# Six tiles of the first layer ahead of the expert steps and two between them, instead of four and four; gates, splits and the last output moved to fit

## The chip, the cores and the metric

One core of one Trainium2 chip. The metric is the device time of one execution in microseconds (us), smaller is better. The engines are TensorE (PE in the rows; PEld is its weight load), VectorE (DVE), ScalarE (ACT), GpSimd (POOL) and SyncE (SP, which here only issues DMAs).

## The reference

The kernel computes two residual layers over x of 32 batches x 128 tokens x 128 channels, all float32:

```python
# layer 0: low-rank conditioned linear, exact gelu; u = v = fside (128 x 16 per batch)
z  = einsum('bfr,bor->bfo', einsum('bfi,bir->bfr', x, v) / 128, u) / 16
x  = x + gelu(x @ W.T + fc_bias + z + cond[:, None, :])
# layer 1: four experts and a shared one, top 2 of 4 per batch
gate_logits = gate_in(means of x over token ranges) @ gate_w + gate_b
gate_logits = gate_logits * (1 + scale) + shift      # scale, shift from silu(cond)
w_be = top-2 weights of softmax(gate_logits)         # one weight per batch and expert
for e in range(4):
    h = gelu_tanh(x @ ew1[e] + eb1[e])               # 128 -> 512
    out += w_be[:, e] * mask[e] * (h @ ew2[e] + eb2[e])  # 512 -> 128
x  = x + out + gelu_tanh(x @ sw1 + sb1) @ sw2 + sb2
```

`mask` leaves a third of the tokens out for experts 2 and 3.

## The kernel before

The 32 batches are 8 tiles of 4 batches, 512 columns each. Every engine has its program written out by hand, so the order of calls in the Python code is the order of each engine's queue, and semaphores tie the queues together.

**Layer 0 of a tile** is `xT` and `transpose_F` (PE transposes of x and of fside), their copies on ScalarE (`xT_copy`, `fT_copy`), `matrices` (PE: F F^T per batch), `matrix` (VectorE, L666: adds W^T), `layer0` (PE, L515), `gelu0` (ScalarE, L355) and `residual` (VectorE, L673). Then x1 is cut into a high part (`x1_high`, ScalarE, L389) and a low part (`x1_low`, VectorE, L678), since every large product is made of three matmuls (`product3`: high x high, high x low, low x high; L456, L457, L458). Weights are cut in the same way: `weight_high` (ScalarE, L330) and `weight_low` (VectorE, L691), ten arrays in the order `WEIGHTS`.

**Steps.** A step k is one tile t with one expert s (0 is the shared one), in the order `STEPS`; there are 40. `first_step(t)` is 2, 7, 12, 17, 22, 27, 32, 36. `up(k)` makes the four 128-row chunks of the hidden layer on PE, `gelu(k)` takes them through ScalarE, `split(k)` cuts them on VectorE (for s = 0 L701 and L705, otherwise L711 and L716, four of each), `down(k)` multiplies back on PE. PE runs `up(k + 2)` ahead of `down(k)`. Five PSUM banks form a ring for `up`.

**Early and late tiles.** The first `NA` = 4 tiles go through layer 0 before `up(0)`; with their own PSUM banks. Tile t >= NA is *late*: its pieces stand between steps, the first at step `first_step(t - NA)` (`late_tile(k, place)` gives the tile whose piece at this place is due in step k), and all of them share PSUM bank 7. Since exact gelu and tanh gelu sit in two function tables of ScalarE, each late tile costs it two table loads (L361 and L380).

**Gates.** `segment_sums` (VectorE, L685) sums x1 over token ranges, `time_gate` and `gate_in` prepare, `logits` (PE, L583) sums over channels, `modulation` reads the product of the conditioning, `gate_logits` and `gate_weights` (VectorE) rank and weigh, `gate_tanh` (ScalarE) is between them. Group 0 is tiles 0 to 3, then 4-5 and 6-7; `late_gate` places the later two. Every `split` of an expert needs the weights `w_be` of its tile.

**Output of a tile:** `out_sum` (VectorE, L728), `out_transpose` (PE, L569), `out_copy` (ScalarE, L398), then a DMA from SP.

`keep_busy` (L462) issues matmuls on ones, whose result is not used. The chunks of x are `CHUNKS` = tiles 0, 1, 2-3, 4-5, 6-7, numbered 0 to 4.

Of the kernel before, what the change touches and what calls it, by code (L numbers as in the profile page):

```python
# [12 lines left out]
def build(nc, x, fside, cond, W, fc_bias, gate_w, gate_b, time_w, time_b,  # L13
# [4 lines left out]
    NB = 4  # L18
# [28 lines left out]
    NA = 4  # L47
# [6 lines left out]
    with ExitStack() as ctx:  # L54
# [122 lines left out]
        psOut = ps[:, 7, :]  # L177

# [55 lines left out]
        def _(sp):  # L234
# [26 lines left out]
            load_weight(WEIGHTS[0])  # L261
            sp.dma_start(b1_rows[0:CH, :], sb1.rearrange("(c p) -> c p", c=CH)).then_inc(b1_in, 16)
            sp.dma_start(b1_rows[CH:NS * CH, :], eb1.rearrange("e (c p) -> (e c) p", c=CH)).then_inc(b1_in, 16)
            for dst, src in (
                    (gate_raw[:, :, :], gate_w.rearrange("(g d) e -> d g e", g=3)),
                    (gate_b_row[:, :], gate_b.rearrange("(a e) -> a e", a=1).to_broadcast([128, E])),
                    (time_w_raw[:, :], time_w)):
                sp.dma_start(dst, src).then_inc(gate_loads_in, 16)
            load_weight(WEIGHTS[1])
            for n in WEIGHTS[2:]:  # L270
                load_weight(n)
            for c in (3, 4):
                load_F(c)
                load_x(c)
            for t in range(NT):
# [3 lines left out]
            sp.wait_ge(out_left, 16 * NT)  # L279
# [40 lines left out]
        def _(act):  # L320
# [91 lines left out]
            for t in range(NA):  # L412
# [4 lines left out]
                if t >= 1:  # L417
                    x1_high(t - 1)
                if t >= 2:
                    weight_high(WEIGHTS[t - 2])  # L420
            x1_high(NA - 1)
            weight_high(WEIGHTS[2])
            weight_high(WEIGHTS[3])
            act.wait_ge(b1_ok, 1)
            gelu(0)
            gate_tanh(0)
            gelu(1)
            for n in WEIGHTS[4:6]:
                weight_high(n)
            for k in range(2, K):  # L430
# [5 lines left out]
                if s == NS - 1:  # L436
                    out_copy(t)
                t = late_tile(k, 2)
# [12 lines left out]
            out_copy(NT - 1)  # L451

        @block.tensor
        def _(pe):
# [186 lines left out]
            out_transpose(NT - 1)  # L641

        @block.vector
        def _(dve):
# [74 lines left out]

            def out_sum(t):  # L720
# [49 lines left out]
            def gate_in(g):  # L770
                b = batches(g)
                n = GATES[g][1] - GATES[g][0]
                dve.wait_ge(segsum_ok, NSEG * GATES[g][1] // 2)
# [66 lines left out]
            for t in range(NA):  # L840
# [3 lines left out]
                if t >= 1:  # L844
                    x1_low(t - 1)
                if t == 2:
                    output_rows()
                    weight_low(WEIGHTS[0])
                    segment_sums(0, 2)
            segment_sums(2, 4)  # L850
            time_gate()
            gate_in(0)
            x1_low(NA - 1)
            dve.wait_ge(bias_in, 16 * 3)
            modulation()
            weight_low(WEIGHTS[1])
            weight_low(WEIGHTS[2])
            gate_logits(0)
            split(0)
            gate_weights(0)  # L860
            weight_low(WEIGHTS[3])
            split(1)
            weight_low(WEIGHTS[4])
            weight_low(WEIGHTS[5])
            for k in range(2, K):
# [7 lines left out]
                if k == 4:  # L873
                    output_biases(0)
                t = late_tile(k, 2)
# [23 lines left out]
            out_sum(NT - 1)  # L899
# [24 lines left out]
```

## Time and profile before

| | us |
|---|---|
| median of 3 runs | 264.66 (263.34 to 264.92) |
| profiled execution | 262.98 |
| its span | 261.3 |
| PE busy in the span | 240.2 (92%) |
| DVE busy | 196.7 (75%) |
| ACT busy | 145.0 (55%) |
| mean granted TensorE clock | 0.993 |

The span runs from the first to the last instruction; 1.7 us of the profiled execution lie around it. Matmuls overlap in the records, so the steps' pace is read from the starts of rows, not from their durations.

### The profile page before, as it was taken

How to read it: one execution, taken by the hardware profiler on the slowest of the kernel's cores; microseconds unless marked ns; L12 is line 12 of the kernel's file. 1: busy time of each engine (PE TensorE's matmuls, PEld its weight loads, DVE VectorE, ACT ScalarE, POOL GpSimd, SP SyncE). 2: the span in 40 equal slices, each digit the busy share in tenths (PEclk: the TensorE clock that was granted, in tenths of full speed). 3: DMA queues.
4: the chain of work that ended last, by engine and by line, in shares of the span. 5: the costliest groups of instructions: out<-in, count | busy, mean ns of one | idle time of the engine just before them, and what ended most of it. 6: DMA issues, size and time to landing. Idle time of an engine off the chain costs nothing.

```text
span 261.3 us, 3479 instructions
## 1 busy us (share of the span) xinstructions
PE 240.2 (92%) x1230; PEld 200.7 (77%) x1230; DVE 196.7 (75%) x450; ACT 145.0 (55%) x270; POOL 15.1 (6%) x39
## 2 busy tenths in 40 slices
PE   8987788999899998999899998998989989999963
PEld 7875466888688877888678877886778879898852
DVE  0259899997689546977796966995799859679761
ACT  3478795353976089552966269544735175545500
POOL 6000000004000020002000020002000100010000
PEclk9999979999999999999999999999999999999999
DMA  6997000000000000100001000100000000100101
GB/s 129 219 292 144 1 0 3 0 0 0 3 21 19 0 3 1 40 3 0 0 1 43 0 0 1 43 0 0 0 17 25 0 0 14 29 0 1 40 3 40
DMA packets 17100, 7.41 MB, mean 28 GB/s; under 512 B 5523, under 2 KB 16443, under 8 KB 17083
## 3 DMA queue, kind: packets, MB, share of 16 engines
q1 hardware_dynamic: 16069, 6.98, 10.8%
q10 hardware_dynamic: 854, 0.18, 0.3%
q8 instruction: 10, 0.16, 0.3%
q0 software_dynamic: 160, 0.02, 0.1%
q14 instruction: 7, 0.06, 0.1%
HBM read 5.09 MB, written 2.10 MB: 28 GB/s over the span
## 4 chain that ended last, share of the span: by engine, by line
PE 67%; ACT 14%; DVE 14%; issue 3%; DVEq 0%; POOL 0%; ACTq 0%; POOLq 0%
PE ps L456 20%; PE ps L458 18%; PE ps L457 18%; ACT h L380 5%; PE ps L503 3%; DVE hs_lo L716 3%; ACT hs_hi L383 3%; DVE hs_lo L705 2%; ACT L380 2%; DVE hs_hi L711 2%; PE ps L473 2%; PE ps L462 2%; PE ps L487 2%; ACT L361 1%; PE ps L569 1%
## 5 line engine op out<-in xcount | busy, mean ns | idle before, releaser
L380 ACT ACTIVATE h<-ps,b_col 128x512 f32<-128x512 f32 (+1 forms) x160 | 92.4, 642 | 64.1 <-PE ps L458 49.4
L716 DVE SCALAR_TENSOR_TENSOR hs_lo<-h,w_be,hs_hi 128x512 fp32r<-128x512 f32 (+1 forms) x128 | 76.2, 656 | 0.0
L456 PE MATMUL ps<-x_hi,W_hi 128*128 128x512 f32 (+1 forms) x160 | 64.3, 402 | 8.2 <-ACT hs_hi L383 4.9
L456 PE MATMUL ps<-hs_hi,W_hi 128*128 128x512 f32 (+1 forms) x160 | 59.2, 370 | 5.2 <-DVE hs_lo L716 2.5
L457 PE MATMUL ps<-x_hi,W_lo 128*128 128x512 f32 (+1 forms) x160 | 59.1, 369 | 0.0
L458 PE MATMUL ps<-x_lo,W_hi 128*128 128x512 f32 (+1 forms) x160 | 59.0, 369 | 0.0
L458 PE MATMUL ps<-hs_lo,W_hi 128*128 128x512 f32 (+1 forms) x160 | 58.5, 365 | 0.0
L457 PE MATMUL ps<-hs_hi,W_lo 128*128 128x512 f32 (+1 forms) x160 | 58.2, 363 | 0.0
L711 DVE TENSOR_SCALAR hs_hi<-h,w_be 128x512 fp32r<-128x512 f32 (+1 forms) x128 | 48.2, 440 | 12.7 <-PE ps L458 6.7
L456 PEld LDWEIGHTS ps<-x_hi,W_hi 128*128 128x128 f32 x160 | 30.4, 190 | 20.4 <-ACT hs_hi L383 10.9
L456 PEld LDWEIGHTS ps<-hs_hi,W_hi 128*128 128x128 f32 x160 | 30.1, 188 | 10.9 <-DVE hs_lo L716 2.8
L458 PEld LDWEIGHTS ps<-x_lo,W_hi 128*128 128x128 f32 x160 | 30.5, 190 | 4.4
L457 PEld LDWEIGHTS ps<-hs_hi,W_lo 128*128 128x128 f32 x160 | 30.1, 188 | 4.0
L458 PEld LDWEIGHTS ps<-hs_lo,W_hi 128*128 128x128 f32 x160 | 30.1, 188 | 4.1
L457 PEld LDWEIGHTS ps<-x_hi,W_lo 128*128 128x128 f32 x160 | 30.6, 192 | 2.9
L315 POOL TENSOR_TENSOR x<-x,bias 128x168 f32<-128x168 f32 (+1 forms) x24 | 11.1, 490 | 213.4 <-DVE hs_lo L716 159.9
L701 DVE CAST hs_hi<-h 128x1024 fp32r<-128x1024 f32 x8 | 5.5, 693 | 20.2 <-ACT h L380 20.2
L398 ACT ACTIVATE x_tok<-ps 128x512 f32<-128x512 f32 x8 | 4.8, 599 | 27.4 <-PE ps L569 27.4
L705 DVE TENSOR_TENSOR hs_lo<-h,hs_hi 128x1024 fp32r<-128x1024 f32 x16 | 18.8, 1218 | 0.0
L334 ACT ACTIVATE x<-ps 128x512 f32<-128x512 f32 x8 | 4.8, 598 | 15.0 <-PE ps L473 15.0
L383 ACT ACTIVATE hs_hi<-ps,b_col 128x512 fp32r<-128x512 f32 x16 | 11.0, 689 | 0.0
L666 DVE SCALAR_TENSOR_TENSOR h<-ps,WT 128x512 f32<-128x512 f32 x4 | 2.7, 687 | 9.3 <-PE ps L503 9.3
(106 smaller groups left out, 175.4 us busy)
## 6 DMA issues: line engine op xcount, KB each, us to landing
W_raw<-in_L_cond_ew SPq DMA_DIRECT2D x8, 256.0 KB, 5.5
out<-x_tok SPq DMA_DIRECT2D x8, 256.0 KB, 2.3
x_tok<-in_x SPq DMA_DIRECT2D x6, 168.0 KB
x_tok<-in_x SPq DMA_DIRECT2D x3, 176.0 KB
W_raw<-in_L_cond_sw SPq DMA_DIRECT2D x2, 256.0 KB, 4.6
x_tok<-in_x SPq DMA_DIRECT2D x3, 84.0 KB
F_raw<-in_fside_Bx1x1024x SPq DMA_DIRECT2D x3, 64.0 KB, 4.7
x_tok<-in_x SPq DMA_DIRECT2D x2, 88.0 KB
```

Source lines behind the costliest of these rows:

```text
L315: nc.gpsimd.tensor_tensor(xb[:, :, at:at + n], xb[:, :, at:at + n], bias2[:, i, t * NB:(t + 1) * NB].unsqueeze(2).to_broadcast([128, NB, n ...
L380: ins = nc.scalar.activation(span(h[:, k % 3, c, :], s), up_bank(k, c), ACT.Gelu_apprx_tanh, bias=b1_col[:, s, c:c + 1])
L383: ins = nc.scalar.activation(hs_hi[:, k % 2, c, :], up_bank(k, c), ACT.Gelu_apprx_tanh, bias=b1_col[:, s, c:c + 1])
L456: nc.tensor.matmul(dst, w_hi, m_hi, start=start, stop=False)
L457: nc.tensor.matmul(dst, w_lo, m_hi, start=False, stop=False)
L458: return nc.tensor.matmul(dst, w_hi, m_lo, start=False, stop=stop)
L462: nc.tensor.matmul(dst, ones[:, :], ones[:, :], start=True, stop=True)
L503: last = nc.tensor.matmul(dst[:, b * D:(b + 1) * D], f[:, b, :], f[:, b, :], start=True, stop=True)
L701: nc.vector.tensor_copy(hs_hi[:, k % 2, CH // 2:, :], h[:, k % 3, CH // 2:, :]).then_inc(shared_hi_ok, 1)
L705: nc.vector.tensor_tensor(hs_lo[:, k % 2, c:c + 2, :], h[:, k % 3, c:c + 2, :], f32(hs_hi[:, k % 2, c:c + 2, :]), ALU.subtract).then_inc(l ...
L711: nc.vector.tensor_scalar(hs_hi[:, k % 2, :, c], h[:, k % 3, :, c], w_be[:, t * NB + b, s - 1:s], None, ALU.mult).then_inc(hi_ok, 1)
L716: nc.vector.scalar_tensor_tensor(hs_lo[:, k % 2, :, c], h[:, k % 3, :, c], w_be[:, t * NB + b, s - 1:s], f32(hs_hi[:, k % 2, :, c]), ALU.m ...
```

## The change

- `NA` becomes 6: tiles 4 and 5 go through layer 0 ahead of `up(0)`, tiles 6 and 7 are late, at steps 2 and 7 on. The gate groups are unchanged, but `late_gate` puts group 1 (tiles 4-5) at steps 3 to 9 instead of 13 to 19, and group 2 (tiles 6-7) at 13 to 19 instead of 23 to 29.
- SP issues the loads in another order: the small loads, then the first weight, then chunk 3 of x and fside, then the other weights, then chunk 4.
- ScalarE makes x1_high of tiles 0 and 1 only in the front; those of tiles 2 and 3 come around `gelu(1)`, those of 4 and 5 after `gelu(4)` and `gelu(5)`. `gelu(1)` now stands ahead of `gate_tanh(0)`, and the weights are cut elsewhere.
- VectorE makes `time_gate` in the front, sums the segments of tiles 0 to 3 in one call (three instructions) and of 4-5 in another, and has `weight_low` and `x1_low` at other places.
- The last tile's output goes in two halves of two batches each, with a PSUM bank, a copy and a DMA for each.

```diff
--- before.py
+++ after.py
@@ -44,7 +44,7 @@
     AT = {step: k for k, step in enumerate(STEPS)}
     RING = [0, 1, 4, 2, 3]
 
-    NA = 4
+    NA = 6
 
     GATES = [(0, 4), (4, 6), (6, 8)]
 
@@ -175,6 +175,7 @@
         psIdle = ps[:, 3, 0:128]
         psY = [ps[:, 5, :], ps[:, 6, :]]
         psOut = ps[:, 7, :]
+        psLast = [psOut, ps[:, RING[0], :]]
 
         block = ctx.enter_context(nc.Block())
 
@@ -258,7 +259,6 @@
             load_x(1)
             load_F(2)
             load_x(2)
-            load_weight(WEIGHTS[0])
             sp.dma_start(b1_rows[0:CH, :], sb1.rearrange("(c p) -> c p", c=CH)).then_inc(b1_in, 16)
             sp.dma_start(b1_rows[CH:NS * CH, :], eb1.rearrange("e (c p) -> (e c) p", c=CH)).then_inc(b1_in, 16)
             for dst, src in (
@@ -266,17 +266,24 @@
                     (gate_b_row[:, :], gate_b.rearrange("(a e) -> a e", a=1).to_broadcast([128, E])),
                     (time_w_raw[:, :], time_w)):
                 sp.dma_start(dst, src).then_inc(gate_loads_in, 16)
+            load_weight(WEIGHTS[0])
+            load_F(3)
+            load_x(3)
             load_weight(WEIGHTS[1])
             for n in WEIGHTS[2:]:
                 load_weight(n)
-            for c in (3, 4):
-                load_F(c)
-                load_x(c)
-            for t in range(NT):
+            load_F(4)
+            load_x(4)
+            for t in range(NT - 1):
                 sp.wait_ge(out_tok_ok, t + 1)
                 sp.dma_start(out[t * NB:(t + 1) * NB, :, :].rearrange("b l d -> l b d"), x_tok[:, t, :, :]
                              ).then_inc(out_left, 16)
-            sp.wait_ge(out_left, 16 * NT)
+            for half in range(2):
+                b = (NT - 1) * NB + half * NB // 2
+                sp.wait_ge(out_tok_ok, NT + half)
+                sp.dma_start(out[b:b + NB // 2, :, :].rearrange("b l d -> l b d"),
+                             x_tok[:, NT - 1, half * NB // 2:(half + 1) * NB // 2, :]).then_inc(out_left, 16)
+            sp.wait_ge(out_left, 16 * (NT + 1))
 
         @block.gpsimd
         def _(pool):
@@ -414,17 +421,18 @@
                     xT_copy(t + 2)
                     fT_copy(t + 2)
                 gelu0(t)
-                if t >= 1:
+                if t in (1, 2):
                     x1_high(t - 1)
-                if t >= 2:
-                    weight_high(WEIGHTS[t - 2])
-            x1_high(NA - 1)
-            weight_high(WEIGHTS[2])
-            weight_high(WEIGHTS[3])
+                if t in (3, 5):
+                    weight_high(WEIGHTS[t // 4])
             act.wait_ge(b1_ok, 1)
             gelu(0)
+            for n in WEIGHTS[2:4]:
+                weight_high(n)
+            x1_high(2)
+            gelu(1)
             gate_tanh(0)
-            gelu(1)
+            x1_high(3)
             for n in WEIGHTS[4:6]:
                 weight_high(n)
             for k in range(2, K):
@@ -435,6 +443,8 @@
                 t, s = STEPS[k - 3] if k >= 3 else (0, 0)
                 if s == NS - 1:
                     out_copy(t)
+                if k in (4, 5):
+                    x1_high(k)
                 t = late_tile(k, 2)
                 if t is not None:
                     fT_late_copy(t)
@@ -448,7 +458,11 @@
                 g = late_gate(k, 7)
                 if g is not None:
                     gate_tanh(g)
-            out_copy(NT - 1)
+            for half in range(2):
+                b = slice(half * NB // 2, (half + 1) * NB // 2)
+                act.wait_ge(out_ps, NT + half)
+                nc.scalar.activation(x_tok[:, NT - 1, b, :], psLast[half].rearrange("p (b d) -> p b d", d=D)[:, b, :],
+                                     ACT.Copy).then_inc(out_tok_ok, 1)
 
         @block.tensor
         def _(pe):
@@ -638,7 +652,18 @@
                 t, s = STEPS[k - 1] if k >= 1 else (0, 0)
                 if s == NS - 1:
                     out_transpose(t)
-            out_transpose(NT - 1)
+
+            t = NT - 1
+            for half in range(2):
+                pe.wait_ge(outT_ok, NSEG * (t + 1 + half))
+                if half == 0:
+                    pe.wait_ge(out_tok_ok, t)
+                else:
+                    pe.wait_ge(h_ok, CH * K)
+                for b in range(half * NB // 2, (half + 1) * NB // 2):
+                    last = nc.tensor.transpose(psLast[half][:, b * D:(b + 1) * D], outT[:, t % 2, b * L:(b + 1) * L],
+                                               ident[:, :])
+                last.then_inc(out_ps, 1)
 
         @block.vector
         def _(dve):
@@ -717,6 +742,19 @@
                                                    w_be[:, t * NB + b, s - 1:s], f32(hs_hi[:, k % 2, :, c]),
                                                    ALU.mult, ALU.subtract).then_inc(lo_ok, 1)
 
+            def last_sum(half):
+                t = NT - 1
+                b = slice(half * NB // 2, (half + 1) * NB // 2)
+                dst_v, sum_v, x1_v = (ap.rearrange("p (b l) -> p b l", l=L)
+                                      for ap in (outT[:, t % 2, :], psY[t % 2], x1[:, t, :]))
+                if half == 0:
+                    dve.wait_ge(down_ok, AT[t, NS - 1] + 1)
+                    dve.wait_ge(x1b_ok, NSEG * NT)
+                    dve.wait_ge(out_ps, t - 1)
+                for at, dst, n in SEGS:
+                    nc.vector.tensor_tensor(dst_v[:, b, dst:dst + n], sum_v[:, b, at:at + n], x1_v[:, b, at:at + n],
+                                            ALU.add).then_inc(outT_ok, 1)
+
             def out_sum(t):
                 dve.wait_ge(down_ok, AT[t, NS - 1] + 1)
                 dve.wait_ge(x1b_ok, NSEG * (t + 1))
@@ -770,7 +808,7 @@
             def gate_in(g):
-                dve.wait_ge(segsum_ok, NSEG * GATES[g][1] // 2)
+                dve.wait_ge(segsum_ok, NSEG * (g + 1))
                 linked(nc.vector.tensor_tensor(gate_terms[:, :, b, :],
                                                segsum[:, :, b].unsqueeze(3).to_broadcast([128, NSEG, n * NB, E]),
                                                gw[:, :, :].unsqueeze(2).to_broadcast([128, NSEG, n * NB, E]), ALU.mult))
@@ -841,25 +879,29 @@
                 if t + 1 < NA:
                     matrix(t + 1)
                 residual(t)
-                if t >= 1:
+                if t in (1, 2):
                     x1_low(t - 1)
+                if t == 1:
+                    time_gate()
                 if t == 2:
                     output_rows()
+                if t == 3:
+                    segment_sums(0, 4)
+                if t == 4:
                     weight_low(WEIGHTS[0])
-                    segment_sums(0, 2)
-            segment_sums(2, 4)
-            time_gate()
+            segment_sums(4, 6)
             gate_in(0)
-            x1_low(NA - 1)
             dve.wait_ge(bias_in, 16 * 3)
             modulation()
             weight_low(WEIGHTS[1])
+            gate_logits(0)
             weight_low(WEIGHTS[2])
-            gate_logits(0)
             split(0)
+            weight_low(WEIGHTS[3])
             gate_weights(0)
-            weight_low(WEIGHTS[3])
+            x1_low(2)
             split(1)
+            x1_low(3)
             weight_low(WEIGHTS[4])
             weight_low(WEIGHTS[5])
             for k in range(2, K):
@@ -872,6 +914,8 @@
                     weight_low(WEIGHTS[2 * k + 3])
                 if k == 4:
                     output_biases(0)
+                if k in (6, 7):
+                    x1_low(k - 2)
                 t = late_tile(k, 2)
                 if t is not None:
                     matrix(t)
@@ -896,7 +940,8 @@
                 g = late_gate(k, 7)
                 if g is not None:
                     output_biases(g)
-            out_sum(NT - 1)
+            last_sum(0)
+            last_sum(1)
 
 
 # ---- launch: one core; inputs and output as the reference has them ----
```

`late_tile` and `late_gate` and the pieces that they place are the same code as before.

The order of VectorE's queue in the front, before the change, from tile 1's residual sum on (`h` is the matrix of layer 0, `x` is x1):

```order
L673 TENSOR_TENSOR x<-x,h 128x512
L678 TENSOR_TENSOR x_lo<-x,x_hi 128x512
L666 SCALAR_TENSOR_TENSOR h<-ps,WT 128x512
L673 TENSOR_TENSOR x<-x,h 128x512
L678 TENSOR_TENSOR x_lo<-x,x_hi 128x512
L752 COPY eb2T<-ps 128x4 x3
L754 COPY b_col<-ps 128x20
L756 MEMSET eb2T 128x1
L757 MEMSET eb2T 128x1
L691 TENSOR_TENSOR W_lo<-W_raw,W_hi 128x512
L685 TENSOR_REDUCE segsum<-x 128x8 x3
L673 TENSOR_TENSOR x<-x,h 128x512
```

The same queue after the change, from the matrix of tile 4 to the gate's input:

```order
L691 SCALAR_TENSOR_TENSOR h<-ps,WT 128x512
L698 TENSOR_TENSOR x<-x,h 128x512
L710 TENSOR_REDUCE segsum<-x 128x16 x3
L691 SCALAR_TENSOR_TENSOR h<-ps,WT 128x512
L698 TENSOR_TENSOR x<-x,h 128x512
L716 TENSOR_TENSOR W_lo<-W_raw,W_hi 128x512
L698 TENSOR_TENSOR x<-x,h 128x512
L710 TENSOR_REDUCE segsum<-x 128x8 x3
L812 TENSOR_TENSOR gate_terms<-segsum,gw 128x3x64
L815 TENSOR_REDUCE gate_fold<-gate_terms 128x64
```

The sums over four tiles (128x16) now stand between the residual sum of tile 3 and the matrix of tile 5, and two residual sums and a second group of sums stand ahead of the gate's input.

ScalarE's queue ahead of the first tanh gelu, before the change (`x_hi` is x1_high, the gelu of layer 0 is the row with `bias`):

```order
L355 ACTIVATE h<-ps,bias 128x128 x4
L389 ACTIVATE x_hi<-x 128x512
L330 ACTIVATE W_hi<-W_raw 128x512
L389 ACTIVATE x_hi<-x 128x512
L330 ACTIVATE W_hi<-W_raw 128x512 x2
L380 ACT_TABLE_LOAD
L380 ACTIVATE h<-ps,b_col 128x512
```

and after it:

```order
L362 ACTIVATE h<-ps,bias 128x128 x4
L337 ACTIVATE W_hi<-W_raw 128x512
L362 ACTIVATE h<-ps,bias 128x128 x8
L337 ACTIVATE W_hi<-W_raw 128x512
L387 ACT_TABLE_LOAD
L387 ACTIVATE h<-ps,b_col 128x512
```

One cut of a weight is left between the last gelu of layer 0 and the table load, in place of three cuts of weights and two of x1.

VectorE's queue between the weights of gate 0 (`w_be`) and the split of step 2, before:

```order
L817 TENSOR_TENSOR w_be<-denom,sum_top 128x64
L691 TENSOR_TENSOR W_lo<-W_raw,W_hi 128x512
L701 CAST hs_hi<-h 128x1024
L705 TENSOR_TENSOR hs_lo<-h,hs_hi 128x1024 x2
L691 TENSOR_TENSOR W_lo<-W_raw,W_hi 128x512 x2
L711 TENSOR_SCALAR hs_hi<-h,w_be 128x4x128 x4
```

and after:

```order
L855 TENSOR_TENSOR w_be<-denom,sum_top 128x64
L703 TENSOR_TENSOR x_lo<-x,x_hi 128x512
L726 CAST hs_hi<-h 128x1024
L730 TENSOR_TENSOR hs_lo<-h,hs_hi 128x1024 x2
L703 TENSOR_TENSOR x_lo<-x,x_hi 128x512
L716 TENSOR_TENSOR W_lo<-W_raw,W_hi 128x512 x2
L736 TENSOR_SCALAR hs_hi<-h,w_be 128x4x128 x4
```

Two cuts of x1 have come into this stretch; the weight cut that stood in it is now ahead of the gate's weights.

## Rows read from the trace of the kernel before

**Rows 1.** Window, us; busy us (x count) of PE, PEld, DVE, ACT, POOL; clock, DMA share, GB/s.

```profile
20.00:60.00 40.00, 35.13 (x163) 27.43 (x162) 38.70 (x98) 25.73 (x48) 1.35 (x3) 0.96 0.11 22
```

**Rows 2.** Window of the first loads, same columns.

```profile
2.00:9.00 7.00, 6.94 (x42) 5.90 (x40) 0.69 (x1) 3.25 (x6) 3.12 (x7) 1.00 0.94 186
```

**Rows 3.** Timeline of the front: start us, us, engine, line, operation [idle before <-releaser].

```profile
11.74 1.06 PE L515 MATMUL ps<-x,h 128*128 128x128 f32 x8
...
14.74 1.06 PE L515 MATMUL ps<-x,h 128*128 128x128 f32 x8
...
18.14 1.14 ACT L355 ACTIVATE h<-ps,bias 128x128 f32<-128x128 f32 x4 [0.64 <-PE ps L515]
...
19.01 1.13 PE L515 MATMUL ps<-x,h 128*128 128x128 f32 x8 [0.91 <-issue]
...
19.98 1.50 PE L462 MATMUL ps<-ones 128*128 128x128 f32 x12
...
21.73 0.50 PE L456 MATMUL ps<-x_hi,W_hi 128*128 128x512 f32 x1 [0.25 <-DVE W_lo L691]
```

**Rows 4.** Timeline from the segment sums to the first gate, same columns.

```profile
24.04 1.33 DVE L685 TENSOR_REDUCE segsum<-x 128x8 f32<-128x336 f32 x3
...
25.25 1.28 ACT L380 ACT_TABLE_LOAD   x1
...
26.54 0.69 ACT L380 ACTIVATE h<-ps,b_col 128x512 f32<-128x512 f32 x1
...
29.25 1.29 DVE L691 TENSOR_TENSOR W_lo<-W_raw,W_hi 128x512 fp32r<-128x512 f32 x2
...
30.88 0.22 DVE L784 TENSOR_TENSOR logit<-ps,gate_mul 128x64 f32<-128x64 f32 x1 [0.34 <-PE ps L583]
```

**Rows 5.** Timeline of split and down of step 2.

```profile
45.90 2.73 DVE L716 SCALAR_TENSOR_TENSOR hs_lo<-h,w_be,hs_hi 128x512 fp32r<-128x512 f32 x4
...
48.77 0.47 PE L456 MATMUL ps<-hs_hi,W_hi 128*128 128x512 f32 x1
```

**Rows 6.** Timeline of split and down of steps 6 (no gate) and 16 (gate 1).

```profile
66.61 0.69 DVE L701 CAST hs_hi<-h 128x1024 fp32r<-128x1024 f32 x1 [2.86 <-ACT h L380]
...
72.92 0.39 PE L456 MATMUL ps<-hs_hi,W_hi 128*128 128x512 f32 x1
...
125.87 0.69 DVE L701 CAST hs_hi<-h 128x1024 fp32r<-128x1024 f32 x1 [3.63 <-ACT h L380]
...
132.71 0.50 PE L456 MATMUL ps<-hs_hi,W_hi 128*128 128x512 f32 x1 [0.37 <-DVE outT L728]
```

**Rows 7.** Timeline, the output transposes of tiles 0 to 5.

```profile
75.69 0.60 PE L569 MATMUL ps<-ident,outT 128*128 128x128 f32 x4
...
105.31 0.60 PE L569 MATMUL ps<-ident,outT 128*128 128x128 f32 x4
...
135.57 0.60 PE L569 MATMUL ps<-ident,outT 128*128 128x128 f32 x4
...
165.23 0.60 PE L569 MATMUL ps<-ident,outT 128*128 128x128 f32 x4
...
193.35 0.60 PE L569 MATMUL ps<-ident,outT 128*128 128x128 f32 x4
...
219.58 0.60 PE L569 MATMUL ps<-ident,outT 128*128 128x128 f32 x4
```

**Rows 8.** Timeline of the end.

```profile
256.39 0.82 DVE L728 TENSOR_TENSOR outT<-ps,x 128x168 f32<-128x168 f32 x3 [3.12 <-PE ps L458]
...
258.58 0.37 SPq L277 DMA_DIRECT2D out<-x_tok  x1
```

**Rows 9.** Windows around the clock's fall (columns of Rows 1).

```profile
32.00:33.00 1.00, 0.00 (x0) 0.00 (x0) 0.97 (x3) 1.00 (x3) 0.00 (x0) 1.00 0.00 0
...
35.00:36.00 1.00, 1.00 (x3) 0.80 (x3) 1.00 (x2) 1.00 (x3) 0.00 (x0) 0.50 0.00 0
...
252.00:253.00 1.00, 0.00 (x0) 0.00 (x0) 1.00 (x2) 0.00 (x0) 0.00 (x0) 1.00 0.00 0
```

## The prediction

> **What bounds the kernel now.** I read the engines' shares first: PE is busy 92% of the span, VectorE 75%, ScalarE 55%, so by the average PE sets the time. Then the windows, because the average is over stages with different limits. Two stages must be told apart. From 20 to 60 us VectorE is busy 38.7 of 40 us and PE 35.1 [rows 1]: this stage belongs to VectorE, which cuts ten weights and four tiles, works out the first gate and starts the splits, all at once. Its last word is step 2: the split of step 2 ends at 45.90 + 2.73 = 48.63 us, and down(2) starts at 48.77 [rows 5]. From there on PE runs without such waits and sets the pace; a block of five steps (from one output transpose to the next) takes 29.62, 30.26, 29.66, 28.12 and 26.23 us [rows 7]. The first three hold a late tile, the fourth a gate without one, the fifth neither. So the sum has three parts: how much later PE reaches the start of down(2), what each block loses or gains, and the end.
>
> **Part 1, the front: when does down(2) start?** I follow the queues, each on the durations of before.
>
> *PE to the layer-0 product of tile 3.* In the front a tile costs PE 3.0 us: the products of tiles 0 and 1 start at 11.74 and 14.74 [rows 3], with the next tile's transposes between them. Now such transposes follow tile 1 too; at 3.0 a tile, tile 2's starts at 17.7, tile 3's at 20.7 and ends at 21.9 (1.13 to 1.16 each). In the kernel before, tile 3's starts at 19.01 [rows 3]. VectorE and ScalarE keep up to here: time_gate adds some 1.3 us to VectorE's queue at tile 1, where it would wait anyway, and its matrix of tile 3 is then ready by about 20.2.
>
> *The sums in the way.* ScalarE's gelu of tile 3 ends 1.14 us after 21.9 plus a hop, at 23.1 [rows 3], the residual sum at 23.7. Behind it VectorE now has the segment sums of four tiles, and only then the matrix of tile 5, for which PE waits. Three sums over two tiles take 1.33 us [rows 4]; three over four tiles take between that and 2.66, and I take 2.4, since the elements double and the fixed part doesn't. The matrix (0.7) thus ends at 26.8 and tile 5's product starts at 26.85, where PE alone would have had it at 24.1: a hole of 2.7 us on PE.
>
> *up(0).* From the start of the last layer-0 product to the end of keep_busy are 21.48 - 19.01 = 2.5 us [rows 3]; up(0) starts at 29.3, against 21.73.
>
> *gelu(0).* Here the new order on ScalarE pays. Before, up(0) began at 21.73 but gelu(0) only at 26.54, 4.8 us later, since ScalarE still had a tile and two weights to cut and then a table to load, 1.28 us from 25.25 [rows 4]. Now ScalarE has one weight to cut after its last layer-0 gelu (29.2 to 29.85), then the load. The load waits for the first chunk of up(0), ready some 0.95 us after 29.3 (three matmuls, the first 0.50 [rows 3]), so it runs 30.3 to 31.55 and gelu(0) starts at 31.6: 5.05 later than before, not 7.6.
>
> *The gate.* up(1) is paced by gelu(0) and logits(0) stands behind it, so the first row of gate_logits(0) moves from 30.88 [rows 4] to 35.95. Its other inputs are ready: residual 5 ends at 29.9, its sums at 31.1, gate_in at 31.95, the conditioning's product after up(0) at 32.65, modulation at 34.0.
>
> *VectorE from there.* Before, 48.63 - 30.88 = 17.75 us without a hole lead to the end of split(2). In the new order the same items stand there, and three more of 0.65 each (two in 1.29 [rows 4]): a weight cut that used to stand ahead of the logits, and the x1_low of tiles 2 and 3. So split(2) ends at 35.95 + 17.75 + 1.95 = 55.65, and down(2) starts at 55.8, against 48.77: **+7.0 us**. As a check from the other side: VectorE's own added work up to here is two matrices, two residual sums and three sums, 4 x 0.65 + 1.3 = 3.9 us; the other 3.1 are holes, in which it waits for tile 5's gelu (1.1), for the conditioning's product (0.7) and for the logits (1.3).
>
> The lower bound of this term is +4.1, if the holes close; the upper is +10.2, if the clock falls in PE's hole (below).
>
> ScalarE's other moves cost nothing here: gelu(1) runs 37.0 to 40.6 behind two weights and one x1_high, while split(1) only needs it at 46.6; that VectorE stretch is its cover, 6 us thick. gate_tanh(0) behind it is done at 40.8, needed at 43.4.
>
> **Part 2, the blocks.** Step numbers name what stands in a block.
>
> - To down(6): before, no gate stands here. From the start of the split of step 6 to down(6) are 72.92 - 66.61 = 6.31 us. With a gate, 132.71 - 125.87 = 6.84, and PE then waits for the output sum behind gate_logits [rows 6]. The new order puts group 1's gate_logits there, and x1_low of tile 4 (0.65) ahead of it: 6.84 + 0.65 - 6.31 = **+1.2**. Lower bound 0 if VectorE has run ahead, upper 2.5, gate_logits whole.
> - Steps 7 to 11, late tile 7 and gate_weights(1): as steps 17 to 21 before, 29.66 for 29.62, nothing.
> - Steps 12 to 16, a gate and no late tile: as steps 22 to 26 before, 28.12 for 30.26, **-2.14**.
> - Steps 17 to 21: nothing of the kind but gate_weights(2), as 27 to 31 before; 26.23 for 29.66, **-3.43**.
> - Steps 22 to 26: 26.23 for 28.12, **-1.89**.
>
> Together -7.46 [rows 7]. These pitches hold everything that a late tile costs: its products on PE and the wait of PE's ring while ScalarE loads tables.
>
> On the table loads the Trainium skill ("ScalarE: Activation LUTs", What ACT_TABLE_LOAD costs) adds to the load of about 1.28 us a drain of 1.38, 2.66 us a switch. By that each of the two tiles taken out of the steps would give back some 2.8 us of ScalarE more, a gain of up to 5.5 us beyond the sum. The trace doesn't agree: the load of 1.28 us starts at 25.25 and the gelu behind it at 26.54 [rows 4], so there is no such drain, and I give that no chance of its own.
>
> **Part 3, the end.** From the last output sum to the issue of the store are 258.58 - 256.39 = 2.2 us, and 2.7 more to the end of the span [rows 8]. In halves the sums cost more (six instructions for three), but the first half's transposes and copy run beside them, and the last copy and store are half as large. No row shows a half; the bounds are +0.3 (fixed costs doubled, nothing overlaps) and -1.3 (half of everything behind the sums); I take -0.6.
>
> **Loads.** Chunk 3 of x is now wanted by PE at 16.9. By 9 us 7 x 186 GB/s = 1.3 MB have come [rows 2], which is chunks 0 to 2 with fside. Behind them stand 0.26 MB of the first weight and 0.59 MB of chunk 3, at the same 186 GB/s 4.6 us, so 13.6; SP has issued them by about 13. That leaves 3 us, so it costs nothing, and the price if it doesn't hold is 1 us for each us late. The weights move back by some 3 us but are wanted later still.
>
> **The sum:** 7.0 + 1.2 - 7.46 - 0.6 = +0.1 on 262.98, the profiled execution, so 263.1. That execution lies 1.7 below the median of 264.66; I add the same 0.1 to the median: **264.8 us**. A measurement of this kernel can tell about 1%, 2.6 us, from no change.
>
> **Rivals.**
>
> 1. *The front is absorbed (faster).* VectorE has 3.1 us of holes by my chain. If its queue runs closer, because the sums over four tiles are short or gelu(0) isn't held by the load, only its own 3.9 us are added, as in a stage that VectorE bounds throughout. Then 264.8 - 3.0 = 261.8. For it speaks VectorE's 97% in this stage before [rows 1]; against it that each hole has a wait of its own. Chance 0.2.
> 2. *The clock falls in PE's hole (slower).* After stretches with PE idle (0.00 busy from 32 to 33) the granted clock was 0.50 at 35, the 1.2 GHz level; yet after an equally empty 252 to 253 it stayed at 1.00 [rows 9]. Before, the fall hid behind VectorE. In the new front a hole of 2.7 us lies just ahead of tile 5's product, keep_busy and up(0)'s first chunk, 1.1 + 1.5 + 0.6 us that would double and push gelu(0): +3.2, so 268.0. It decides if the clock is at 0.5 between 27 and 30 us. The Trainium skill ("TensorE: Matmul & The Clock Gate", Part 1: The HAM clock gate) says that the gate halves the clock after an idle window and that the windows run free of the kernel; by that a hole either meets one or not. The trace shows both outcomes, so it agrees. Chance 0.15. A later fall, in PE's idle time from 36 to 40 before up(2), is likelier still, but VectorE hides it: down(0) may come 1.4 later, down(1) doesn't wait for it.
> 3. *Chunk 3 is late.* If its small pieces and the weight come at half the rate of [rows 2], the 0.85 MB take 9.1 us from 9 on, so 18.1, 1.2 late: 266.0. Chance 0.1.
> 4. *The change doesn't do what it says in the blocks*: late tiles 6 and 7 meet both gates' work on VectorE in steps 2 to 11, and 2 us of new waits eat the savings: 266.8. Chance 0.05.
>
> The forecast itself has 0.5. Its own range is 263.2 to 266.4 (the sums 1.4 to 2.66, the end -1.3 to +0.3, the gate 0 to 2.5, not all at once). The range that holds 8 in 10 takes in rival 1's and most of rival 2's: 261.6 to 267.6. Faster by over 1% (below 262.0): most of rival 1 and a little of the forecast, 0.22. Slower by over 1% (above 267.3): rival 2 and a little of 4, 0.17. Within: 0.61.
>
> **What would show it.** A hole on PE of 2 to 3 us at 24 to 27, ended by the matrix of VectorE behind the sums; the table load starting only after up(0)'s first chunk; gelu(0) near 31.6; down(2) near 55.8; the pitches of output transposes near 29.7, 28.1, 26.2, 26.2, 26.2. I am wrong in part 1 if down(2) comes before 54 or after 58, in part 2 if the second pitch stays near 30, and on the loads if PE's transposes of tile 4 wait.

## The result, and the profile after

The changed kernel takes 265.86 us in the median of 13 runs (263.9 to 266.64), the kernel before 264.01 (262.88 to 264.95) beside it. The ratio is 1.006, with a 95% interval of 1.0039 to 1.0081: a little slower, inside the range and inside the 1% that was forecast as no change. The medians lie 1.85 us apart where the sum said 0.1. The profiled execution took 265.67 us, its span 263.9 for 261.3. Of the runs below one is left out: the profiled one of sums_and_fill_end took 342.63 us at a mean granted clock of 0.652.

The front, in the timeline of the changed kernel (start us, us, engine, line, operation, idle before and its releaser):

```profile
16.85 0.66 PE L487 MATMUL ps<-ident,x_tok 128*128 128x128 f32 x4
...
20.78 1.06 PE L529 MATMUL ps<-x,h 128*128 128x128 f32 x8
...
22.85 1.16 PE L529 MATMUL ps<-x,h 128*128 128x128 f32 x8
...
23.78 2.41 DVE L710 TENSOR_REDUCE segsum<-x 128x16 f32<-128x672 f32 x3
...
26.10 0.68 DVE L691 SCALAR_TENSOR_TENSOR h<-ps,WT 128x512 f32<-128x512 f32 x1
...
26.88 2.04 PE L529 MATMUL ps<-x,h 128*128 128x128 f32 x8 [2.87 <-issue]
...
28.72 1.99 PE L476 MATMUL ps<-ones 128*128 128x128 f32 x12
...
30.46 0.47 PE L470 MATMUL ps<-x_hi,W_hi 128*128 128x512 f32 x1
...
31.48 1.28 ACT L387 ACT_TABLE_LOAD   x1 [0.85 <-PE ps L472]
...
32.77 0.69 ACT L387 ACTIVATE h<-ps,b_col 128x512 f32<-128x512 f32 x1
...
37.12 0.23 DVE L822 TENSOR_TENSOR logit<-ps,gate_mul 128x64 f32<-128x64 f32 x1 [1.02 <-PE ps L597]
...
41.17 0.80 PE L470 MATMUL ps<-x_hi,W_hi 128*128 128x512 f32 x1 [4.09 <-DVE W_lo L716]
...
56.83 0.47 PE L470 MATMUL ps<-hs_hi,W_hi 128*128 128x512 f32 x1 [0.26 <-DVE hs_lo L741]
```

Read it from the top. PE doesn't wait for the x of tile 4. The rows at 20.78, 22.85 and 26.88 are the layer-0 products of tiles 3, 4 and 5. The segment sums fill VectorE from 23.78, the matrix of tile 5 stands behind them, and PE, idle for 2.87 us, starts that tile's product at 26.88. "Issue" hides the releaser in this row; what names it is that the matrix ends 0.1 us earlier. The product then takes 2.04 us, its neighbour 1.16, and keep_busy 1.99 where it took 1.50 [rows 3]. The table load starts only behind up(0)'s first chunk. The last row is down(2), at 56.83 for 48.77 [rows 5].

The windows of the same kernel over the three stretches in which PE waited or had just waited (window, busy us with counts of PE, PEld, DVE, ACT, POOL, granted clock, DMA share, GB/s):

```profile
26.60:29.60 3.00, 2.72 (x13) 2.75 (x14) 1.38 (x3) 0.64 (x3) 0.00 (x0) 0.50 0.00 0
40.00:46.60 6.60, 5.43 (x13) 4.28 (x14) 6.33 (x16) 5.03 (x10) 0.00 (x0) 0.50 0.00 0
...
254.00:262.00 8.00, 5.42 (x16) 3.72 (x16) 2.06 (x8) 0.77 (x2) 0.00 (x0) 0.79 0.00 0
```

So the clock fell three times to its 1.2 GHz level, behind each of three waits of PE of 2.5 to 4.1 us; in the profiled execution of before it fell once, at 33 to 37 us [rows 9]. The wait that the fall of before followed was the shorter of the two that the prediction compares:

```profile
33.37 0.78 PE L456 MATMUL ps<-x_hi,W_hi 128*128 128x512 f32 x1 [1.78 <-ACT hs_hi L383]
...
253.32 0.50 PE L456 MATMUL ps<-hs_hi,W_hi 128*128 128x512 f32 x1 [2.55 <-DVE hs_lo L716]
```

A wait of 1.78 us met a fall and one of 2.55 us none, so the length of the last wait doesn't settle it alone.

The output transposes of tiles 0 to 5, timeline, for [rows 7]:

```profile
84.98 0.60 PE L583 MATMUL ps<-ident,outT 128*128 128x128 f32 x4
114.61 0.60 PE L583 MATMUL ps<-ident,outT 128*128 128x128 f32 x4
142.70 0.60 PE L583 MATMUL ps<-ident,outT 128*128 128x128 f32 x4
168.92 0.60 PE L583 MATMUL ps<-ident,outT 128*128 128x128 f32 x4
195.14 0.60 PE L583 MATMUL ps<-ident,outT 128*128 128x128 f32 x4
221.36 0.60 PE L583 MATMUL ps<-ident,outT 128*128 128x128 f32 x4
```

The blocks take 29.63, 28.09, 26.22, 26.22 and 26.22 us, for 29.62, 30.26, 29.66, 28.12 and 26.23 before. And the end, for [rows 8]:

```profile
255.10 0.80 PE L470 MATMUL ps<-hs_hi,W_hi 128*128 128x512 f32 x1 [2.54 <-DVE hs_lo L741]
...
259.69 1.01 DVE L755 TENSOR_TENSOR outT<-ps,x 128x84 f32<-128x84 f32 x6 [4.64 <-PE ps L472]
260.30 0.90 PE L664 MATMUL ps<-ident,outT 128*128 128x128 f32 x4 [0.65 <-DVE outT L755]
...
261.18 0.89 SPq L284 DMA_DIRECT2D out<-x_tok  x2
```

From the start of the output sums to the end of the span are 263.9 - 259.69 = 4.2 us, for 261.3 - 256.39 = 4.9. But the last down, from 255.10 to the sums, takes 4.6 us; the same matmuls take 3.1 where the clock holds (see fill_end).

The two spans differ by 2.6 us, and the marks account for it: front +8.06 (down(2)), up to tile 0's output transpose (84.98 - 56.83) - (75.69 - 48.77) = +1.23, blocks -7.51, last down +1.5, end -0.7.

### The profile page after: what moved, and what is told of

It reads as the page before. It is cut to its first block, busy times and chain, and to the rows that moved or that the text cites. A ratio compares the mean times of both kernels' runs of the same rounds, so it can differ in the third digit from the quotient of the medians.

```text
span 263.9 us, 3473 instructions
## 1 busy us (share of the span) xinstructions
PE 241.8 (92%) x1230; PEld 204.7 (78%) x1230; DVE 197.2 (75%) x450; ACT 140.5 (53%) x265; POOL 15.1 (6%) x39
## 4 chain that ended last, share of the span: by engine, by line
PE 75%; DVE 12%; ACT 7%; issue 4%; POOL 0%; DVEq 0%; ACTq 0%; POOLq 0%
PE ps L470 22%; PE ps L472 20%; PE ps L471 20%; ACT h L387 4%; PE ps L517 3%; PE ps L529 3%; PE ps L476 2%; DVE hs_lo L730 2%; ACT hs_hi L390 2%; PE ps L487 2%; DVE hs_lo L741 2%; PE ps L501 1%; DVE hs_hi L736 1%; PE ps L583 1%; DVE W_lo L716 1%
## 5 line engine op out<-in xcount | busy, mean ns | idle before, releaser
L470 PE MATMUL ps<-x_hi,W_hi 128*128 128x512 f32 (+1 forms) x160 | 63.1, 394 | 9.5 <-DVE W_lo L716 4.1
L470 PE MATMUL ps<-hs_hi,W_hi 128*128 128x512 f32 (+1 forms) x160 | 59.8, 373 | 5.2 <-DVE hs_lo L741 2.8
L405 ACT ACTIVATE x_tok<-ps 128x512 f32<-128x512 f32 x7 | 4.2, 598 | 19.6 <-PE ps L583 19.6
L691 DVE SCALAR_TENSOR_TENSOR h<-ps,WT 128x512 f32<-128x512 f32 x6 | 4.1, 688 | 9.2 <-PE ps L517 9.2
```

Of the source, the lines that this page charges most:

```text
L470: nc.tensor.matmul(dst, w_hi, m_hi, start=start, stop=False)
```

## The experiments

All but two start from the changed kernel, and are compared with its 265.86 us; ratios are to the kernel before, run beside each. The changed kernel was not run again beside them, and the median of the kernel before lay between 263.03 and 264.09 from one batch of runs to the next. So a difference of about 1 us between medians of two batches shows little by itself; the rows of the profiles have to carry it.

The profiled executions also differ in when the front gets going: where the loads come as in the changed kernel, the product of tile 3 starts between 20.41 and 21.17 us. In every one that has the hole, tile 5's product starts 6.1 us behind it. So what a step costs in the front is counted below from the start of tile 3's product.

**The hole on PE: the sums moved behind the matrix.**

```diff
-                if t == 3:
-                    segment_sums(0, 4)
                 if t == 4:
                     weight_low(WEIGHTS[0])
+                    segment_sums(0, 4)
```

> The changed kernel with the segment sums of tiles 0 to 3 moved in VectorE's queue from ahead of the matrix of tile 5 to behind the weight cut that up(0) needs. My theory of the front: the 2.41 us of sums make the hole of 2.9 us on PE, that delays tile 5's gelu, up(0), the table load, gelu(0), the logits, and only then VectorE's full stretch. Then the hole shrinks to about 0.5 us, up(0) starts near 27 for 30.46, gelu(0) near 29.2 for 32.77, the first row of gate_logits(0) near 33.6 for 37.12, down(2) near 53.3 for 56.83, and the time falls by 3.5 us, below the kernel before. The rival, that VectorE's amount of work sets the front whatever its order, gives no change, within 0.5 us. A third, that only the fall of the clock in the hole costs, gives 1.1.

Measured: 261.44 us (260.01 to 262.11), ratio to the kernel before 0.9899 (0.9864 to 0.9933). Its timeline:

```profile
20.41 1.06 PE L529 MATMUL ps<-x,h 128*128 128x128 f32 x8
...
24.07 1.13 PE L529 MATMUL ps<-x,h 128*128 128x128 f32 x8 [0.43 <-issue]
...
26.06 2.40 DVE L710 TENSOR_REDUCE segsum<-x 128x16 f32<-128x672 f32 x3
...
26.30 0.48 PE L470 MATMUL ps<-x_hi,W_hi 128*128 128x512 f32 x1
...
28.62 0.69 ACT L387 ACTIVATE h<-ps,b_col 128x512 f32<-128x512 f32 x1
...
32.99 0.22 DVE L822 TENSOR_TENSOR logit<-ps,gate_mul 128x64 f32<-128x64 f32 x1
...
52.70 0.47 PE L470 MATMUL ps<-hs_hi,W_hi 128*128 128x512 f32 x1 [0.65 <-DVE hs_lo L741]
```

The hole is 0.43 us, the product takes 1.13 again, gelu(0) comes 4.15 earlier and down(2) 4.13. This front had started 0.37 earlier; from tile 3's product to down(2) are 32.29 us for 36.05, so the order of the queue is worth 3.8. Of these, 2.44 are the shorter hole, and the rest is what the fall behind it costs (next experiment). VectorE does exactly the same work; only its place in the queue has changed. So the rival that the amount of work sets the front falls, and so does the third, since 3.8 us is more than the 1.1 that it allowed for the clock's fall alone.

**The clock in that hole: filled with matmuls.**

```diff
+                if t == NA - 1:
+                    keep_busy(10, ps[:, 6, 0:128])
                 layer0(t)
```

> The changed kernel with ten matmuls on ones, whose result isn't used, ahead of tile 5's layer-0 product, so that PE works through the hole of 2.9 us. In the changed kernel's trace the granted clock is 0.50 from 26.6 to 29.6, the product takes 2.04 us instead of 1.1 and keep_busy 1.99 instead of 1.5. If the idle hole makes the clock fall, it stays at 1.00 there, up(0) starts 1.1 us earlier, near 29.3, and the time falls by 1.1. If the clock falls for another reason, nothing changes. The hole itself stays, since VectorE's matrix ends it.

Measured: 264.12 us (263.06 to 265.24), 1.7 below the changed kernel; ratio to before 1.0008 (0.9987 to 1.0029), clear of the changed kernel's 1.006 (1.0039 to 1.0081). Its timeline, and the window from 26.6 to 29.6, for the first of the windows above:

```profile
20.65 1.06 PE L529 MATMUL ps<-x,h 128*128 128x128 f32 x8
...
26.75 1.13 PE L529 MATMUL ps<-x,h 128*128 128x128 f32 x8 [0.64 <-issue]
...
55.34 0.47 PE L470 MATMUL ps<-hs_hi,W_hi 128*128 128x512 f32 x1 [0.68 <-DVE hs_lo L743]
```

```profile
26.60:29.60 3.00, 2.85 (x23) 2.79 (x24) 1.76 (x4) 1.66 (x5) 0.00 (x0) 1.00 0.00 0
```

The clock holds, the product takes 1.13, and up(0), at 28.98, and down(2) start 1.5 us earlier. Counted from tile 3's product, down(2) comes after 34.69 us for 36.05. Idle PE made the clock fall, and the fall cost 1.4 us here because the whole chain to gelu(0) was behind it: 0.9 in tile 5's product and 0.5 in keep_busy.

**The clock in the last wait: filled in both kernels.**

```diff
+                if k == K - 1:
+                    pe.wait_ge(out_tok_ok, NT - 1)
+                    keep_busy(9, psOut[:, 0:128])
                 down(k)
```

In the changed kernel:

> The changed kernel with nine matmuls on ones, whose result isn't used, ahead of the last down, in the 2.54 us in which PE waits for the last split. In the profiled execution of the changed kernel the clock was at the lower level in that down, which took 4.5 us from its first to its last row for 3.0 in that of before, where the same wait went by without a fall. If the fall meets some executions and not others, the median falls by up to 1.5 us and the runs lie closer together than the 263.9 to 266.6 of the changed kernel. If it meets none but the profiled one, nothing changes.

and in the kernel before:

> The kernel before with nine matmuls on ones ahead of the last down, as in the run on the changed kernel. Its 13 runs lie in two heaps, 262.9 to 263.4 and 263.9 to 265.0. If the upper heap are executions in which the clock falls in the last wait, this kernel's runs all lie in the lower one, and the median falls by 0.5 to 1 us. If the heaps come from elsewhere, nothing changes.

Measured: 264.78 us (264.0 to 265.3, 12 runs) for the changed kernel, 1.1 below it by the medians and closer together; by the ratio, 1.0036 (1.0015 to 1.0056), it is 0.6 below, and the intervals overlap. For the kernel before 263.11, against 263.03 unfilled beside it: the median didn't fall by the 0.5 to 1 us expected, since most of the unfilled runs of this batch are low anyway. But all 12 filled runs lie between 262.75 and 263.45, where the 17 unfilled ones lie at 262.91 to 263.16 (eleven) and 264.57 to 265.03 (six). The upper heap is gone. The profiles say what it was: without the filling, six of nine show a fall in the last down, which then takes 4.4 to 4.7 us, and three show none, and 3.1. One of the six is a kernel with the front of before (halves_only, below). The end of the filled changed kernel:

```profile
252.27 2.17 PE L476 MATMUL ps<-ones 128*128 128x128 f32 x18
254.97 0.50 PE L470 MATMUL ps<-hs_hi,W_hi 128*128 128x512 f32 x1 [0.53 <-DVE hs_lo L744]
...
258.04 1.01 DVE L758 TENSOR_TENSOR outT<-ps,x 128x84 f32<-128x84 f32 x6 [3.12 <-PE ps L472]
```

The last down takes 258.04 - 254.97 = 3.1 us for 4.6. Its front still had the fall, which this time came a little later: tile 5's product took 1.13, up(0) began at 29.68 with a first matmul of 0.77, gelu(0) came at 32.68. From tile 3's product to gelu(0) are 10.64 us with the hole filled, 11.99 in the changed kernel and 12.16 here; in the other profiles with the hole unfilled they are 12.25 to 13.27. So the fall costs 1.4 to 2.6, by how much of the chain lies in its stretch.

**The clock ahead of up(2).**

```diff
+                if k == 0:
+                    keep_busy(14, ps[:, 6, 0:128])
                 if k + 2 < K:
                     up(k + 2)
```

> The changed kernel with fourteen matmuls on ones ahead of up(2), in the 4.09 us in which PE waits for the weight cut behind gate_logits(0). In the changed kernel's trace the granted clock is 0.50 from 40 to 46.6 there, and up(2) takes 5.3 us for 2.8. My theory: this second fall is hidden, since split(2) on VectorE, not PE, sets the start of down(2) at 56.8. Then the clock stays at 1.00, down(0) starts some 2.4 us earlier, down(2) stays within 0.2 us, and the time doesn't change. If every fall of the clock costs what it takes from PE, the time falls by 2.4.

Measured: 266.1 us (263.89 to 266.69), the same as the changed kernel. Windows of this kernel, from the filled wait through up(2):

```profile
37.00:41.00 4.00, 3.31 (x30) 3.12 (x28) 3.56 (x11) 4.00 (x8) 0.00 (x0) 1.00 0.02 4
41.00:44.00 3.00, 2.78 (x12) 2.17 (x12) 3.00 (x5) 3.00 (x7) 0.00 (x0) 1.00 0.00 0
```

The clock holds through up(2), down(0) starts at 44.18 for 46.46, and down(2) at 56.87 for 56.83. The longest of the three falls, 6.6 us at half clock, costs nothing, since VectorE's split(2) ends last.

**ScalarE's order undone in part.**

```diff
             act.wait_ge(b1_ok, 1)
-            gelu(0)
             for n in WEIGHTS[2:4]:
                 weight_high(n)
             x1_high(2)
+            gelu(0)
             gelu(1)
```

> The changed kernel with two weight cuts and the x1_high of tile 2 put back ahead of gelu(0) on ScalarE, as they stood in the kernel before. They take 1.18 + 0.66 us and ScalarE waits 0.9 us there for up(0) now. My theory, that gelu(0) paces up(1) and with it the logits and VectorE, gives gelu(0), gate_logits(0) and down(2) each 0.9 to 1.0 us later and the time 1 us longer. If ScalarE's order is covered, nothing changes.

Measured: 265.99 us (265.19 to 266.71), within 0.2 of the changed kernel; ratio to before 1.009 (1.0057 to 1.0122), which overlaps with the changed kernel's. Its timeline:

```profile
29.62 1.68 ACT L337 ACTIVATE W_hi<-W_raw 128x512 fp32r<-128x512 f32 x3
...
31.18 0.64 ACT L396 ACTIVATE x_hi<-x 128x512 fp32r<-128x512 f32 x1
...
31.64 0.39 PE L472 MATMUL ps<-x_lo,W_hi 128*128 128x512 f32 x1
...
31.84 1.28 ACT L387 ACT_TABLE_LOAD   x1
```

The load starts at 31.84 for 31.48, gelu(0) 0.36 later, down(2) at 57.25, 0.4 later. My 0.9 to 1.0 is missed. I had taken only ScalarE's wait of 0.85 as cover for cuts of 1.84; here up(0) itself came 0.3 later, with the clock low from 26 to past 31, so that nearly all of the cuts ran while up(0)'s first chunk was awaited anyway. Against up(0), which starts at 30.78, gelu(0) has moved by less than 0.1 us. So the order as such is worth next to nothing beside a falling clock; without the fall it might be worth more, which I haven't run. Nor have I run the other way to shorten this chain: in the late tiles a one-column gelu stands ahead of gelu0_late's waits, and the load of 1.28 us carries its line (L368); gelu(0) has none ahead of it, though ScalarE is idle for 0.85 us there.

**Chunk 3 of x behind six more weights.**

```diff
+            for n in WEIGHTS[1:7]:
+                load_weight(n)
             load_F(3)
             load_x(3)
-            load_weight(WEIGHTS[1])
-            for n in WEIGHTS[2:]:
+            for n in WEIGHTS[7:]:
                 load_weight(n)
```

> The changed kernel with chunk 3 of x and fside issued behind six more weights, 1.57 MB. By the rates of the loads (280 GB/s for weights, 186 for x) it lands near 18.6 us, PE wants it at 16.85, so PE waits 1.8 us there and the time grows by about 1.8. If the order of the loads has more room than I reckoned, nothing changes; if everything waits for the last of the loads, it grows by 3 or more.

Measured: 273.05 us (272.7 to 275.3), 7.2 above. SP's issues of the chunk's x, the transposes of tile 4, and the windows of that wait and behind the next:

```profile
12.70 4.38 SPq L239 DMA_DIRECT2D x_tok<-in_x  x3
...
21.05 1.11 PE L488 MATMUL ps<-ident,x_tok 128*128 128x128 f32 x4 [4.75 <-DMA x_tok<-in_x]
```

```profile
17.00:21.00 4.00, 0.00 (x0) 0.00 (x0) 2.37 (x9) 0.00 (x0) 0.00 (x0) 0.60 0.98 236
...
22.00:24.00 2.00, 2.00 (x11) 1.77 (x10) 0.00 (x0) 1.18 (x2) 0.00 (x0) 0.50 0.83 168
...
33.00:36.00 3.00, 3.00 (x15) 3.00 (x16) 0.86 (x2) 1.15 (x5) 0.00 (x0) 0.50 0.00 0
```

The chunk came at 21.05, not 18.6: my reckoning by rates was 2.4 us short. If the prediction's was short by as much, its room of 3 us is less than 1. That isn't measured: SP's three issues of the chunk take 4.38 us here, to 17.08, and 1.68 in the changed kernel, to 11.36, so part of the 2.4 may belong to this order alone. And a late load costs more than its lateness: 4.2 us late at the first row, 5.9 at tile 3's product, 6.6 at up(0) (37.03), 7.2 at down(2), as the clock falls in the load's wait and again behind the sums.

**x1_low of tiles 4 and 5 one step later.**

```diff
-                if k in (6, 7):
-                    x1_low(k - 2)
+                if k in (7, 8):
+                    x1_low(k - 3)
```

> The changed kernel with the x1_low of tiles 4 and 5 one step later, behind the splits of steps 7 and 8, so that it doesn't stand ahead of gate_logits(1) and the output sum of tile 0. From down(2) to the output transpose of tile 0 the changed kernel takes 28.15 us, 1.23 more than before. If 0.6 of that is the x1_low in VectorE's queue, this stretch takes 27.5 and the time falls by 0.6; if PE's wait of 1.0 us there has another cause, nothing changes.

Measured: 264.77 us (264.32 to 265.86), 1.1 below the changed kernel by the medians, 0.5 by the ratio of 1.0041 (1.002 to 1.0063), whose interval overlaps with the changed kernel's. In the profile PE's wait at down(6) is shorter; the changed kernel's row, then those of this one:

```profile
82.11 0.51 PE L470 MATMUL ps<-hs_hi,W_hi 128*128 128x512 f32 x1 [0.98 <-DVE outT L766]
```

```profile
82.15 0.50 PE L470 MATMUL ps<-hs_hi,W_hi 128*128 128x512 f32 x1 [0.38 <-DVE outT L766]
...
85.02 0.60 PE L583 MATMUL ps<-ident,outT 128*128 128x128 f32 x4
```

0.38 us for 0.98, and from down(2) (57.48) to the transpose 27.54 us for 28.15: the expected 0.6. The medians' other 0.5 is no more than medians of two batches differ by.

**The halves alone, on the kernel before.** The diff is that of the change for `last_sum`, `psLast`, the last transposes, copies and stores.

> The kernel before, with the last tile's output in two halves and nothing else of the change. In the changed kernel the stretch from the last output sum to the end of the span is 4.2 us for 4.9 before. If that is all that the halves do, this kernel is 0.7 us faster than before (0.3%). If the shorter end came from the rest of the change, or if splitting the store costs what it gives back, it is within 0.2 us of before.

Measured: 263.64 us (262.15 to 264.27), ratio 0.9985 (0.9965 to 1.0006). By the profile the end takes 262.1 - 257.90 = 4.2 us as in the changed kernel; by the times a gain of 0.4 that the interval doesn't part from none. Its profiled execution also met the fall in the last down, 257.90 - 253.26 = 4.6 us behind a wait of 2.54, with nothing of the change in its front:

```profile
253.26 0.50 PE L466 MATMUL ps<-hs_hi,W_hi 128*128 128x512 f32 x1 [2.54 <-DVE hs_lo L737]
...
257.90 1.01 DVE L751 TENSOR_TENSOR outT<-ps,x 128x84 f32<-128x84 f32 x6 [4.70 <-PE ps L468]
```

**Together.** Sums behind the matrix and the last wait filled:

> The changed kernel with both the sums behind the matrix and the nine matmuls ahead of the last down. If the two causes add, the time is that of sums_behind_matrix less what fill_end gave, some 4 to 4.5 us below the changed kernel and 2 to 2.5 below the kernel before. If the fall of the clock at the end is only moved about, it is that of sums_behind_matrix.

Measured: 260.38 us (259.91 to 260.87, five runs), ratio 0.9878 (0.9844 to 0.9912): 5.5 below the changed kernel and 2.65 below the kernel before. The two causes add, 4.4 and 1.1 by the medians; the 4 to 4.5 of the expectation was too small a sum of them. With x1_low one step later as well:

> The changed kernel with the sums behind the matrix, the nine matmuls ahead of the last down and x1_low one step later. If the three add up, it is 0.6 us below sums_and_fill_end, near 259.9, and 1.4% below the kernel before. If taking one wait away only opens another, it is the same as sums_and_fill_end, near 260.5.

Measured: 259.76 us (259.21 to 260.03), ratio 0.9837 (0.9807 to 0.9867), the fastest here: 4.3 us below the kernel before, 6.1 below the changed one. up(0) starts at 26.91, down(2) at 53.32, and from down(2) to the first output transpose are 27.54 us, as in x1_low_later.

## Why the prediction was nearly right, and where not

**Part 1, the front, +7.0.** Each row of the chain came where it was put, up to the hole: the sums 2.41 for 2.4, the matrix's end 26.78 for 26.8, tile 5's product 26.88 for 26.85. sums_behind_matrix shows that this hole was the cause and not VectorE's load. From the product on everything is 1.0 to 1.2 late: up(0) 30.46 for 29.3, gelu(0) 32.77 for 31.6, logits 37.12 for 35.95, down(2) 56.83 for 55.8, so +8.06. With the clock held (fill_front), down(2) comes at 55.34; the pure chain was thus sized 0.5 too high, the fall adds 1.4, and the rest is the later start of this execution's front. That the two errors point in opposite ways is luck. (The lower bound of this term should have been 7.0 - 3.1 = 3.9, not 4.1.)

**Rival 2 was no rival but part of the course.** I gave the fall in PE's hole 0.15 and a price of 3.2. It came in the front of every profile with that hole unfilled (the changed kernel, fill_end, fill_middle, scalar_cuts_first, x1_low_later, chunk3_later), six of six. It cost 1.4 in the changed kernel, because the clock was back within the chain and didn't double all of it, and up to 2.6 in the others. The step that failed is the one where I set one fall against one non-fall [rows 9] and took the second as a reason for the sum at full clock. The range, too, was said to take in most of this rival, but ended at 267.6 with the rival priced at 268.0.

**The last down was left out altogether.** "After an equally empty 252 to 253 it stayed at 1.00" was one execution. before_fill_end and the profile of halves_only show that the same wait meets a fall in a good part of the executions of the kernel before, 1.5 us each; its median already holds some of that. So of the 2.6 us between the two profiled spans 1.5 are chance: the profiled execution of before escaped this fall. In the changed kernel the runs suggest that it is commoner (12 of 13 lie 1.5 us or more above the lowest, 263.9), but that its share is larger than before's isn't shown.

**ScalarE's new order "pays".** That gelu(0) is 6.2 later and not 8.7 like up(0) was rightly read; that the order of the cuts causes it isn't shown: with two weights and an x1_high put back (scalar_cuts_first), gelu(0) kept its distance from up(0) within 0.1 us. There up(0) itself is late enough to cover them.

**Part 2.** down(6) +1.2, measured +1.23, and the x1_low in it is 0.6 (x1_low_later). Blocks -7.46, measured -7.51. The gain that the prediction mentions beyond the sum, for a drain at the table loads, couldn't have come on top in any case: whatever a load costs is in the pitches, which were taken whole. That a block's pitch can be carried from one place to another that holds the same pieces was the safest step of all.

**Part 3.** -0.6, measured -0.7 in the profile, on the kernel before alone 0.4 with no interval clear of zero.

**Loads.** "It costs nothing" was right; the room behind it may have been overrated (chunk3_later).

Rival 1 (the front absorbed) can be had, but by an order that the change doesn't have. Rivals 3 and 4 didn't come.

## What to carry to other kernels

When work is moved ahead of the steady stage, list what each queue now holds between the last producer and the first consumer: 2.4 us of sums, needed by nobody for another 6 us, stood ahead of a matrix that PE waited for and cost 3.8. Price a wait of TensorE's as the wait and the slow stretch behind it, and ask for each whether another engine ends last there: of three falls of the clock here two cost 1.4 and 1.5 us and the longest nothing. A profile is one execution; where the times lie in two heaps, look for a wait whose clock falls in some executions and not in others, before reading a non-fall as a rule.

## What the runs showed of the hardware

- PE's waits of 2.5 us ahead of the last down, behind a stage fully busy, met a fall of the granted clock to the 1.2 GHz level in six profiles and none in three; the same matmuls took 4.4 to 4.7 us for 3.1. The hole of 2.87 us in the front met one in six of six, and one of 1.78 us did in the kernel before. Dummy matmuls in a wait, leaving 0.5 to 0.9 us idle, kept the clock at 2.4 GHz through it in the five profiles read that have them.
- ScalarE's table load ahead of gelu(0) took 1.28 us, and gelu(0) began within 0.02 us of its end. In the changed kernel the load began only after up(0)'s first chunk had come (31.48, "0.85 <-PE"). In scalar_cuts_first it began at 31.84, 0.20 us after the start of the chunk's third matmul, where the other profiles with that matmul at the full clock have 0.47 to 0.48. So whether a load waits for what its activation waits for stays open.
- Three sums over 672 elements took 2.41 us, over 336 elements 1.33.
